# Softmax sums applied behind the value products: a windowed-attention and ternary feed-forward kernel on one core

## The reference

```python
x = x + attn(layernorm(x), Wq, Wk, Wv, Wo)      # 16 heads of 16, causal, window of 64 keys
x = x + ffn(layernorm(x), W1, b1, W2, b2)
# attn: scores = q k^T / 4 + bias;  softmax(scores) @ v;  @ Wo^T
# ffn:  weights made ternary by gamma = mean|W|, clip(round(W / (gamma + 1e-5)), -1, 1)
#       relu(x @ W1q^T + b1) @ W2q^T + b2,  256 -> 1024 -> 256
```

## Time and profile before

| | |
|---|---|
| median of three runs | 692.78 us |
| profiled execution, span from first to last instruction | 690.4 us |
| PE busy | 649.0 us (94%) |
| DVE busy | 628.3 us (91%) |
| ACT busy | 623.9 us (90%) |
| POOL busy | 618.0 us (90%) |
| DMA queue of SP | 487,160 packets, 50.82 MB |

### The profile page before, as it was taken

The page is one execution under the profiler, slowest core; times in us unless marked ns, Lnnn a source line. Parts: engine busy times, 40 slices in busy tenths (PEclk is TensorE's granted clock), DMA queues, the critical chain, the costliest instruction groups (busy, mean ns, idle before and its releaser), DMA issues.

```text
span 690.4 us, 24485 instructions
## 1 busy us (share of the span) xinstructions
PE 649.0 (94%) x8048; PEld 552.7 (80%) x8048; DVE 628.3 (91%) x1596; ACT 623.9 (90%) x2649; POOL 618.0 (90%) x869
## 2 busy tenths in 40 slices
PE   7668699999999999999999999999999999998887
PEld 5446488888888888888888888887888888887776
DVE  5779889999999999999999999999999999899864
ACT  5689899999999999999999999998999999898833
POOL 7388999999999999999999999999899999999930
PEclk9879989999999999999999999999999999999999
DMA  8576656465756656475756657475665646464000
GB/s 293 80 98 103 75 96 73 77 86 74 125 73 99 98 99 95 77 95 72 128 68 101 96 92 105 51 117 74 102 91 99 74 82 71 61 93 70 18 31 31
DMA packets 497988, 61.17 MB, mean 89 GB/s; under 512 B 470724, under 2 KB 493510, under 8 KB 497864
## 3 DMA queue, kind: packets, MB, share of 16 engines
q1 hardware_dynamic: 487160, 50.82, 51.2%
q10 hardware_dynamic: 10704, 8.80, 4.2%
HBM read 11.86 MB, written 8.39 MB: 29 GB/s over the span
## 4 chain that ended last, share of the span: by engine, by line
PE 40%; POOL 32%; issue 10%; ACT 9%; DVE 6%; DMA 1%; SPq 0%; POOLq 0%; DVEq 0%; ACTq 0%
POOL p L393 13%; POOL tl L417 10%; PE ps L1089 9%; PE ps L1077 7%; ACT p L496 6%; PE ps L987 5%; POOL th L411 5%; PE ps L967 5%; PE ps L1024 4%; PE ps L1035 3%; PE ps L1050 3%; ACT hTh L573 1%; PE ps L1062 1%; POOL rstdC L386 1%; PE ps L960 1%
## 5 line engine op out<-in xcount | busy, mean ns | idle before, releaser
L496 ACT ACTIVATE p<-ps,negm 128x96 f32<-128x96 f32 x1024 | 340.3, 375 | 8.4 <-DVE negm L711 7.7
L417 POOL TENSOR_TENSOR tl<-pt,th 128x384 f16<-128x384 f32 x256 | 234.6, 916 | 16.3 <-ACT th L505 1.8
L496 ACT ACTIVATION_READ_ACCUMULATOR p<-ps,negm 128x1 f32 x1024 | 248.5, 244 | 0.0
L393 POOL TENSOR_TENSOR p<-p,rden 128x384 f32<-128x384 f32 x256 | 214.3, 837 | 7.3 <-DVE rden L718 6.9
L724 DVE STREAM_TRANSPOSE pt<-p 128x384 f32<-128x384 f32 x256 | 141.5, 553 | 14.3 <-POOL p L393 12.9
L711 DVE TENSOR_REDUCE negm<-ps 128x4 f32<-128x384 f32 x256 | 136.0, 531 | 10.4 <-PE ps L967 8.1
L967 PE MATMUL ps<-k,qbd 128*128 128x96 f16 x1536 | 125.2, 208 | 0.0
L967 PEld LDWEIGHTS ps<-k,qbd 128*128 128x128 f16 x1536 | 106.0, 99 | 9.6
L987 PE MATMUL ps<-th,vb 128*128 128x96 f16 (+1 forms) x1120 | 97.1, 202 | 1.8 <-POOL tl L417 1.8
L1077 PE MATMUL ps<-xTCh,w1T 128*128 128x256 f16 x512 | 97.6, 272 | 0.8 <-ACT xTCh L568 0.8
L573 ACT ACTIVATE hTh<-ps 128x512 f16<-128x512 f32 x128 | 79.6, 623 | 19.9 <-PE ps L1077 19.7
(11 more groups left out here) (139 smaller groups left out, 1486.7 us busy)
## 6 DMA issues: line engine op xcount, KB each, us to landing
k<-kst SPq DMA_DIRECT2D x32, 288.0 KB, 4.1
vb<-vd SPq DMA_DIRECT2D x256, 32.0 KB, 2.6
out<-x SPq DMA_DIRECT2D x32, 256.0 KB, 2.5
qbd<-qs SPq DMA_DIRECT2D x254, 32.0 KB, 2.3
x<-in_L_attn_hidden ACTq DMA_DIRECT2D x15, 512.0 KB, 5.4
kw<-kst SPq DMA_DIRECT2D x31, 192.0 KB, 3.8
k<-kst SPq DMA_DIRECT2D x31, 144.0 KB, 3.4
vb<-in_L_ffn_W SPq DMA_DIRECT2D x2, 1024.0 KB, 7.6
```

What stands on the lines that cost most here:

```text
L393: e.tensor_tensor(p3, p3, rden[n % 4][:, :].unsqueeze(2).to_broadcast([128, 4, 96]), ALU.mult).then_inc(s_nm, 1)
L417: e.tensor_tensor(tl[g % 2][:, o], pt[n % 3][:, :], th[g % 2][:, o], ALU.subtract).then_inc(s_lo, 1)
L496: ins = e.activation(p[:, 96 * u:96 * u + 96], bank[:, 96 * u:96 * u + 96], ACT.Exp, bias=m[:, u:u + 1], accum_out=r[:, u:u + 1])
```

## The change

The probabilities are no longer normalized. `exps` writes its sums into a tile for half a chunk (8 blocks, 128 x 32). When all 8 are there (slot 9 of a half, `R_INV`), DVE takes one reciprocal of 128 x 32 and transposes it in 32 x 32 blocks (`turn_inverse`). SP writes this 16 KB tile to main memory (`park_r`, `R_PARK`) and reads it back with two DMAs of 64 rows by 2 KB, which repeat each row for 16 partitions (`widen_r`, `R_WIDEN`), into `rwide`, 128 x 512. POOL multiplies half of `osum` by it (`o_norm`, slot 13 of a half, `R_MUL`). `o_split` and `o_high` now wait for `o_norm`. The transposition and the split come one slot earlier, the value products too (`PV_LAG` 9 to 8), POOL makes all high parts (`high` and `ROUNDED` are gone), and the two pieces of the value projection move from slots 8 and 12 to 10 and 13. The staging tile of the biases, `bt`, now lies in `hT`.

```diff
-A_T, A_Q, A_K, A_V = (1, 2), (6, 14), (6, 15), (8, 12)
+A_T, A_Q, A_K, A_V = (1, 2), (6, 14), (6, 15), (10, 13)
-PV_LAG, O_ADD, O_SPLIT0, O_SPLIT1 = 9, 10, 17, 10
-L_MAX, L_EXP, L_INV, L_NORM, L_TURN, L_PART = 0, 1, 2, 2, 3, 4
+PV_LAG, O_ADD, O_SPLIT0, O_SPLIT1 = 8, 9, 17, 10
+R_INV, R_PARK, R_WIDEN, R_MUL = 9, 10, 12, 13
+L_MAX, L_EXP, L_TURN, L_PART = 0, 1, 2, 3
+def pair_at(n, lag):
+    h, r = divmod(n - lag, 8)
+    return divmod(h, 2) if r == 0 and 0 <= h < 2 * NCH else None
+            def park_r(c, t):
+                e.wait_ge(s_rt, 2 * c + t + 1)
+                if c >= 1:
+                    e.wait_ge(d_r[t], 32 * c)
+                e.dma_start(parked[t], rturn[t][:, :]).then_inc(d_p[t], 16)
+            def widen_r(c, t):
+                e.wait_ge(d_p[t], 16 * (c + 1))
+                if c >= 1:
+                    e.wait_ge(s_on, 2 * (c - 1) + t + 1)
+                for g in range(2):
+                    e.dma_start(rwide[t][64 * g:64 * g + 64, :],
+                                bass.AP(tensor=parked[t].tensor, offset=512 * g, ap=[[1024, 4], [0, 16], [1, 512]])
+                                ).then_inc(d_r[t], 16)
@@ the loop of SP: behind place_q and place_k, ahead of place_v and store
+                ct = pair_at(n, R_PARK)
+                if ct is not None:
+                    park_r(*ct)
+                ct = pair_at(n, R_WIDEN)
+                if ct is not None:
+                    widen_r(*ct)
@@ POOL
-            def norm(n):
-                e.wait_ge(s_rd, n + 1)
-                e.tensor_tensor(p3, p3, rden[n % 4][:, :].unsqueeze(2).to_broadcast([128, 4, 96]),
-                                ALU.mult).then_inc(s_nm, 1)
+            def o_norm(c, t):
+                e.wait_ge(d_r[t], 32 * (c + 1))
+                e.wait_ge(s_osum, 4 * c + 2 * t + 2)
+                e.tensor_tensor(osum[:, t, :], osum[:, t, :], rwide[t][:, :], ALU.mult).then_inc(s_on, 1)
             def o_split(c):
-                e.wait_ge(s_osum, 4 * c + 2)
+                e.wait_ge(s_on, 2 * c + 1)
@@ ACT
             def o_high(c):
-                e.wait_ge(s_osum, 4 * c + 4)
+                e.wait_ge(s_on, 2 * c + 2)
@@ DVE
+            def inverse(c, t):
+                e.wait_ge(s_ex, 16 * c + 8 * t + 8)
+                e.reciprocal(rden[t][:, :], rsum[t][:, :, :, :].rearrange("p g i u -> p (g i u)")).then_inc(s_rd, 1)
+            def turn_inverse(c, t):
+                e.wait_ge(s_rd, 2 * c + t + 1)
+                e.transpose(rturn[t][:, :], rden[t][:, :]).then_inc(s_rt, 1)
```

More of the change, by code:

```diff
@@ L29 @@
 X_LATE = (6, 17, 25)
-PV_LAG, O_ADD, O_SPLIT0, O_SPLIT1 = 9, 10, 17, 10
-ROUNDED = (0, 1, 4, 5, 7, 9, 10, 12, 13, 14, 15)
-L_MAX, L_EXP, L_INV, L_NORM, L_TURN, L_PART = 0, 1, 2, 2, 3, 4
+PV_LAG, O_ADD, O_SPLIT0, O_SPLIT1 = 8, 9, 17, 10
+R_INV, R_PARK, R_WIDEN, R_MUL = 9, 10, 12, 13
+L_MAX, L_EXP, L_TURN, L_PART = 0, 1, 2, 3
 NP = 3
@@ L41 @@
 SLOTS = range(-44, NQ + 48)
-def rounded(n):
-    return n // 16 * (16 - len(ROUNDED)) + sum(q not in ROUNDED for q in range(n % 16 + 1))
 def chunk_at(n, pos, first):
@@ L178, in build @@
         negm = [sb(f"negm{i}", [128, 4], f32) for i in range(4)]
-        rsum = [sb(f"rsum{i}", [128, 4], f32) for i in range(4)]
-        rden = [sb(f"rden{i}", [128, 4], f32) for i in range(4)]
+        rsum = [sb(f"rsum{t}", [128, 2, 4, 4], f32) for t in range(2)]
+        rden = [sb(f"rden{t}", [128, 32], f32) for t in range(2)]
+        rturn = [sb(f"rturn{t}", [128, 32], f32) for t in range(2)]
+        rwide = [sb(f"rwide{t}", [128, CH], f32) for t in range(2)]
         th = [sb(f"th{i}", [128, 1600], f16) for i in range(2)]
@@ L186, in build @@
         hT = [sb(f"hT{p}", [128, 8, CH // 2], f16) for p in "hl"]
-        bt = sb("bt", [128, F + D], f32)
         gpart = sb("gpart", [128, 2, 2], f32)
@@ L191, in build @@
         nthr = sb("nthr", [128, 2], f32)
+        parked = [nc.dram_tensor(f"parked{t}", (128, 32), f32, kind="Internal").ap() for t in range(2)]
         banks = [ctx.enter_context(nc.psum_tensor(f"ps{i}", [128, 512], f32)) for i in range(8)]
@@ L203, in build @@
         d_out = [sem(f"d_out{i}") for i in range(2)]
+        d_p, d_r = ([sem(f"{n}{t}") for t in range(2)] for n in ("d_p", "d_r"))
         s_sc, s_pv, s_a, s_c = sem("s_sc"), sem("s_pv"), sem("s_a"), sem("s_c")
         s_wp, s_tp, s_gt, s_fp = sem("s_wp"), sem("s_tp"), sem("s_gt"), sem("s_fp")
-        s_mx, s_rd, s_tr = sem("s_mx"), sem("s_rd"), sem("s_tr")
+        s_mx, s_rd, s_rt, s_on, s_tr = sem("s_mx"), sem("s_rd"), sem("s_rt"), sem("s_on"), sem("s_tr")
         s_alo, s_cdv, s_osum, s_olo1 = sem("s_alo"), sem("s_cdv"), sem("s_osum"), sem("s_olo1")
@@ L216, in build @@
         s_fe = sem("s_fe")
-        s_ex, s_hi, s_ahi, s_chi = sem("s_ex"), sem("s_hi"), sem("s_ahi"), sem("s_chi")
+        s_ex, s_ahi, s_chi = sem("s_ex"), sem("s_ahi"), sem("s_chi")
         s_oc, s_ohi, s_whi, s_abs, s_mask = sem("s_oc"), sem("s_ohi"), sem("s_whi"), sem("s_abs"), sem("s_mask")
-        s_nm, s_lo, s_powA, s_rsA, s_powC, s_rsC = (
-            sem("s_nm"), sem("s_lo"), sem("s_powA"), sem("s_rsA"), sem("s_powC"), sem("s_rsC"))
+        s_lo, s_powA, s_rsA, s_powC, s_rsC = (
+            sem("s_lo"), sem("s_powA"), sem("s_rsA"), sem("s_powC"), sem("s_rsC"))
         s_car, s_oh0, s_olo0, s_hp = sem("s_car"), sem("s_oh0"), sem("s_olo0"), sem("s_hp")
@@ L231, in build @@
         smask, kmask = pr[0][:, 0:64].bitcast(f16), pr[0][:, 64:112].bitcast(f16)
+        bt = (hT[0][:, :, :].rearrange("p a b -> p (a b)").bitcast(f32), hT[1][:, 0:2, :].rearrange("p a b -> p (a b)").bitcast(f32))
         below = hT[1][:, 4:8, :].rearrange("p a b -> p (a b)").bitcast(f32)
@@ L315, in _ @@
             for r in (0, 32):
-                e.dma_start(bt[r:r + 1, 0:F], b1_d.rearrange("(a n) -> a n", a=1)).then_inc(d_b, 16)
-                e.dma_start(bt[r:r + 1, F:], b2_d.rearrange("(a n) -> a n", a=1)).then_inc(d_b, 16)
+                e.dma_start(bt[0][r:r + 1, :], b1_d.rearrange("(a n) -> a n", a=1)).then_inc(d_b, 16)
+                e.dma_start(bt[1][r:r + 1, :], b2_d.rearrange("(a n) -> a n", a=1)).then_inc(d_b, 16)
             e.dma_start(n1, w1_d.rearrange("(t p) d -> p t d", p=128)).then_inc(d_w["1"], 16)
@@ L341, in clear_keys_and_queries @@
             def clear_keys_and_queries():
-                e.memset(bt[:, :], 0.0).then_inc(s_bz, 1)
+                e.memset(bt[0][:, :], 0.0)
+                e.memset(bt[1][:, :], 0.0).then_inc(s_bz, 1)
                 for t in range(2):
@@ L369, in biases @@
                 e.wait_ge(d_b, 64)
-                e.tensor_copy(bp[:, :], bt[:, :]).then_inc(s_bh, 1)
+                e.tensor_copy(bp[:, 0:F], bt[0][:, :])
+                e.tensor_copy(bp[:, F:], bt[1][:, :]).then_inc(s_bh, 1)
             def rstd_a(c):
@@ L406, in low @@
                 o = slice(384 * (n % 4), 384 * (n % 4) + 384)
[L407 to L416, removed]
+                e.wait_ge(s_tr, n + 1)
+                if g >= 2:
+                    e.wait_ge(s_pv, g - 1)
+                e.tensor_copy(th[g % 2][:, o], pt[n % 3][:, :]).then_inc(s_hp, 1)
+                e.wait_ge(s_hp, n + 1)
                 e.tensor_tensor(tl[g % 2][:, o], pt[n % 3][:, :], th[g % 2][:, o], ALU.subtract).then_inc(s_lo, 1)
@@ L447, in _ @@
                     low(n - L_PART)
-                if 0 <= n - L_NORM < NQ:
-                    norm(n - L_NORM)
+                ct = pair_at(n, R_MUL)
+                if ct is not None:
+                    o_norm(*ct)
                 gg = group_at(n, O_SPLIT0)
@@ L478, in magnitudes @@
                 e.wait_ge(d_w["1" if j < 2 else "2"], 16)
+                if j == 0:
+                    e.wait_ge(s_bias, 1)
                 w = (n1 if j < 2 else n2).rearrange("p a b -> p (a b)")[:, 1024 * (j % 2):1024 * (j % 2) + 1024]
@@ L488, in exps @@
             def exps(n):
-                p, r, m, bank = pr[n % NP], rsum[n % 4], negm[n % 4], sbank[n % 3]
+                p, m, bank = pr[n % NP], negm[n % 4], sbank[n % 3]
+                r = rsum[n // 8 % 2][:, n // 4 % 2, n % 4, :]
                 e.wait_ge(s_mx, n + 1)
@@ L492, in exps @@
                     e.wait_ge(s_tr, n - NP + 1)
-                if n >= 4:
-                    e.wait_ge(s_rd, n - 3)
+                if n >= 16:
+                    e.wait_ge(s_rd, n // 8 - 1)
                 for u in range(4):
@@ L498, in exps @@
                 ins.then_inc(s_ex, 1)
[L500 to L506, removed]
             def a_norm(c, u):
@@ L604, in _ @@
                     load_x(c + NX)
-                if 0 <= n - L_PART < NQ and (n - L_PART) % 16 not in ROUNDED:
-                    high(n - L_PART)
                 gg = values_at(n, PV_LAG + 1)
@@ L677, in bias_low @@
                 e.wait_ge(s_bh, 1)
-                e.tensor_tensor(bp[32:64, :], bt[32:64, :], bp[32:64, :], ALU.subtract).then_inc(s_bias, 1)
+                e.tensor_tensor(bp[32:64, 0:F], bt[0][32:64, :], bp[32:64, 0:F], ALU.subtract)
```

(17 more changed lines are left out.)

1 line of the change is left out of this document (removed).

## The result

| | before | after |
|---|---|---|
| median, us | 692.21 (691.34 to 693.37, 4 runs) | 907.73 (902.78 to 912.14, 4 runs) |
| span of the profiled execution | 690.4 | 907.9 |
| mean granted clock | 0.983 | 0.883 |

The ratio is 1.311, interval 1.306 to 1.316: 215.5 us slower. Forecast were 873, range 765 to 920.

What follows compares the result with a forecast made beforehand. PE is full and SP's DMA queue equally so; the read-back behind q1 lengthens the chunk loop from 39.2 to 51.05 us. First wo piece at 95.3, 14 periods, then 58.3 and 2.5, plus 2.4: 873 us, range 765 to 920.

Steps and rivals of the forecast that it cites:

- The marks named ahead: Signs of being right: PE waits 7 to 11 us before wo, chunks 48 to 54 us apart, idle near 20%.
- T: On SP, the end of q1's last issue in a chunk; forecast at 87.7 us in chunk 0.
- T to wo0: From T to PE's first wo piece: read-back lands at T + 4.5, then product and split; 7.6 us.
- four rings: Rival: read-back uses only 4 of 16 DMA engines, lands at T + 7.0; time 910 us, chance 0.2.
- wo0 to block 8: On PE, from the first wo piece to score block 8: 1.3 us.
- block 8 to value DMAs: From score block 8 to the first value DMA: 14.1 us plus 2.73 for the later projection, 16.85.
- The clock: PE's granted clock halves after its idle wait; 2.5 us lost per chunk, between 0 and 4.
- Value DMAs: SP's 16 value DMAs in a chunk: 14.3 us.
- from their end to the next T: On SP, from the last value DMA's end to T: 0.5 us for park plus 8.0.
- Relief: POOL loses 214 us of normalization, ACT and DVE some work; worth 0 in the middle, perhaps a few us at ends.
- faster: Rival: POOL's relief shortens PE's waits by 8.5 us if the read-back is issued in time; 684 us, chance 0.05.
- Only the old loop: Rival: read-back reaches POOL in time, only the loop through q1 grows, about 3.0 us a chunk; 739 us, chance 0.09.

Runs made afterwards that it cites:

- e4: The changed kernel with SP's read-back of half 1 directly behind its park, ahead of k1 and q1: 827.74 us, ratio 1.194.
- e1: The changed kernel with the value projection back in slots 8 and 12: 871.05 us, ratio 1.257.
- e3: The changed kernel without park and read-back DMAs, osum multiplied by a tile of ones: 738.66 us, ratio 1.066.
- e9: The changed kernel with each half's read-back as eight DMAs of 16 rows, each from one row: 906.98 us, ratio 1.310.
- e7: The changed kernel with 100 extra matmuls on PE ahead of the first wo piece, in all chunks but the last: 884.44 us, ratio 1.277.
- e13: The changed kernel without park and read-back, osum multiplied by ones, and the value projection back in slots 8 and 12: 696.25 us, ratio 1.004.
- e5: The changed kernel with park and read-back issued by ACT instead of SP, in the same slots: 794.70 us, ratio 1.147.
- e6: e5 with the value projection back in slots 8 and 12: 734.75 us, ratio 1.061.
- e12: e10 with its trip still issued by ACT, but POOL multiplies by ones and never waits for the read-back: 722.30 us, ratio 1.041.
- e10: e6 with four park DMAs in destination-row order and one read-back DMA from 8 rows per half: 728.76 us, ratio 1.050.
- e2: The kernel before with only the value projection moved to slots 10 and 13: 754.78 us, ratio 1.089.

## Why the prediction was right

The mechanism is the one forecast: a loop of one chunk through SP, in which the read-back is asked for behind q1. The marks named ahead are there in kind: PE's wait ahead of the first `wo` put down to the split, POOL's product waiting for a DMA, the clock at 0.50 from within each wait on. Their sizes lie at the upper edge or above it: the waits are 9.2 to 13.5 us (forecast 7 to 11), the chunks 49.3 to 55.0 us apart, six of 14 over the 54 forecast (48 to 54), PE's idle share 24% (near 20%). e4 shows the place (80 us for two issues moved), e1 the projection (37), e3 that the trip is 169 of the 215. Between forecast (span 870.8) and measured (907.9) lie 37 us: 3.3 in front of wo0 of chunk 0 (98.59 against 95.3), 29.9 in 14 loops (53.19 each, 843.22 for wo0 of chunk 14, against 51.05), 3.9 behind it (64.7 against 60.8). Term by term, means over the 14 loops. The 35 us by which the time was missed are such sizes, several of them on one side, and the range held them:

- *T to wo0: 7.6 forecast, 9.2 measured.* Two causes. The landing: POOL's product starts 5.5 us behind T, not 4.5. The condition of the rival "four rings", to which I gave 0.2, seems to hold: while the read-back alone moves, the DMA engines are busy 0.24 of their time, and in e9, with sources that repeat one row 16 times, the data comes 1.4 us behind the last issue, where with four rows it comes 4.2 behind. That agrees with the page "DMA: Bandwidth & Descriptors" of the Trainium skill, section on why a DMA increments its semaphore by 16, which makes the number of DMA engines depend on what divides the slowest dimension of both sides; the traces show the landings and the mean share, not which engines moved the data. But I priced the rival at T + 7.0 by the 512 KB row, and the product starts at T + 5.5, so 1.0 us of its 2.5 is there. That its 910 is nearer to the 907.7 measured than my 873 is luck: of the 35 us between, the landing is some 15, and the other terms below are the rest. The split: I had POOL's pair of `oTh` and `oTl` on the path and ACT and DVE "beside". It is the other way round. DVE's `oTl` ended at 257.23, POOL's at 256.69, since DVE's took 1.64 us where its mean before was 0.975. That puts 0.5 us on the path.
- *wo0 to block 8: 1.3 forecast, 2.5 measured*, and *block 8 to value DMAs: 16.85 forecast, 19.06 measured*. The clock was a term of its own, 2.5 us. e7 takes it apart: at full clock these two are 1.31 and 18.2. So the clock costs 1.2 + 0.9 = 2.1 us a loop, a little under the 2.5; by the distance of wo0 (51.3 us in e7) it is 1.9. The 16.85 was too small by 1.35: in e13, with the projection in its old slot, the way is already 15.0 and not 14.1, and the move of a slot adds 3.2. The mis-sized parts are two. The 2.73 us of PE's work that I added are there, but the second piece of the projection starts 3.3 us later than before (13.74 behind block 8 in a chunk of e7, 10.44 in that of the earlier trace rows), as PE waits for `xTCl` ahead of the feed-forward (15 times in after, up to 0.4 us). And the time from the projection's end to the first value DMA, which I left as it was, grew from 2.35 to 3.2 us.
- *Value DMAs 14.3 forecast, 13.9 measured; from their end to the next T 8.5 and 8.4.* Both held.
- *Relief 0.* e13 shows it: 696.25 against 694.0. The rival "faster" (684) falls by this and not only by SP's queue: it said that from a timely read-back on the change costs nothing and gains 8.5 us. No kernel's median came out below before.
- *Only the old loop, 739.* It was a rival's price, and e3 measured 738.66 for the kernel in which that is what is left. That it fits to the microsecond is luck: the price has 0.5 us a chunk for park, which e3 does not issue, and 2.73 for the projection, where the way grew by 4.5 (14.33 to 18.88). In e3 PE's wait ahead of q1 stays, as the earlier trace rows had it: block 8 starts 1.7 us behind T in 11 of 15 chunks.

In the two misses behind the prediction, e5 and e6, I took ACT's queue for free, since ACT was busy 90% and then less. For e6, 38 us over e13, e12 shows 26 us for a trip that nobody waits for, and e10 that less waiting for the landing is worth 6. e5 lies 56 us over e3; that its value DMAs take 1.8 us more in a chunk is a part of it, and why they do was not tried.

## What to carry over

Where a queue of DMA issues is as long as the critical engine's work, a new transfer is priced by its place in that queue: ask when the queue gets there, and what must have ended first, before asking for bytes. The same round trip cost 169 us with the read-back of half 1 behind the queries, 89 with it ahead of them, and 38 to 56 on another engine's queue (e6, e5). And an operation that is taken from a nearly full engine is worth nothing where another is full, while its replacement may put a wait of a whole transfer ahead of that one.

## What the runs showed that was not expected

- A wait of 2.2 to 4.2 us of PE once in a chunk (e2) already brings 0.50 for 3.4 to 6.8 us in 10 of 11 cases, so that a late transfer costs more than its lateness; the 9 to 13.5 us waits of after bring it for 10.2 to 13.7 us, most of this time while PE still stands.
- DVE and POOL held each other up, and the one that started first ran at its own length. In all 16 chunks of after POOL's `oTl` (128 x 512, its usual 1.16 us) starts 0.06 us ahead of DVE's, which then takes 1.64 us and ends 0.54 behind POOL's; the POOL instruction behind starts meanwhile, and where it is the cast it takes 0.97 us (256.63 to 257.60), where the mean of its kind is 0.53. In 14 of 16 chunks of e13 DVE's `oTl` starts first, by 0.13 to 0.25 us: it takes 0.69 to 0.71 us, and POOL's `tl` takes 1.24 to 1.33 where the mean of its kind is 0.94 (the rows below). So neither the busy time of the one alone nor its kind tells the loss, and the order of the two starts does. The page "GPSIMD Engine Reference" of the Trainium skill, section Specifications, says that GpSimd's way to SBUF is shared with VectorE and contended by its instructions with two SBUF inputs. `oTl` is one, and both traces agree; the section gives no price.

```profile
282.63 0.69 DVE L806 TENSOR_TENSOR oTl<-osum,oTh 128x512 f16<-128x512 f32 x1 [0.68 <-ACT oTh L548]
282.76 1.33 POOL L438 TENSOR_TENSOR tl<-pt,th 128x384 f16<-128x384 f32 x1
```

- Eight DMAs of 32 KB that each repeat one row end no later than two of 128 KB with four source rows, though their issues take 3.8 us instead of 1.2 (e9).
